# Attention probabilities and values in 32 bits: one product for three, one copy for two

## The reference, cut

```python
# cross-attention (layers 0 and 1): 16 heads of 16
scores = jnp.einsum('bhqd,bhkd->bhqk', Q, K) / SCALE
attn = jax.nn.softmax(scores, axis=-1)
out = jnp.einsum('bhqk,bhkd->bhqd', attn, V)
...
# layer 0's feed-forward attention: 16 heads of 64, values mixed from 8 experts
v = jnp.einsum('bthe,bted->bhtd', mix_v, proj_v)
scores = jnp.einsum('bhid,bhjd->bhij', q * scale, k)
probs = jax.nn.softmax(scores, axis=-1)
attn = jnp.einsum('bhij,bhjd->bihd', probs, v)
...
x = x + jnp.tanh(g_xattn[0]) * _L0_xattn_ref(_layernorm(x, axis=-1), ctx_1024, ctx_1024, ...)
x = x + jnp.tanh(g_ffn[0]) * _L0_ffn_ref(_layernorm(x, axis=-1), ...)
x = x + jnp.tanh(g_xattn[1]) * _L1_xattn_ref(_layernorm(x, axis=-1), ctx_1024, ctx_1024, ...)
x = x + jnp.tanh(g_ffn[1]) * _L1_ffn_ref(_layernorm(x, axis=-1), ...)
```

## Time and profile before

| | us |
|---|---|
| median of three runs | 1442.24 |
| lowest, highest | 1440.13, 1442.91 |
| span of the profiled execution | 1442.0 |

### The profile page before, as it was taken

How to read it: one execution, slowest core, us unless ns; L and a number is a source line. 1 busy time by engine, 2 the same in 40 slices (tenths; PEclk the granted TensorE clock), 3 DMA queues, 4 the chain that set the end, 5 groups by cost and what they waited for, 6 DMA issues and landing times. The chain is left out here.

```text
span 1442.0 us, 35263 instructions
## 1 busy us (share of the span) xinstructions
PE 1253.7 (87%) x13822; PEld 996.9 (69%) x13822; DVE 1135.6 (79%) x2068; ACT 903.7 (63%) x2071; POOL 278.4 (19%) x242
## 2 busy tenths in 40 slices
PE   1599998589989899889938999994699999999996
PEld 1376666367767767667725676763489999899995
DVE  5578887689999999999643777777688888888884
ACT  1477875158667677667624667663277677677762
POOL 2000000100000000000000000000236666666663
PEclk8689999799999999999666999995599999999998
DMA  8000000133452353352220000000867788778871
GB/s 231 12 9 9 6 2 2 41 93 74 114 146 67 101 151 76 100 151 73 68 66 9 5 9 5 2 2 1 290 225 227 227 249 245 222 231 250 234 189 30
DMA packets 172065, 152.96 MB, mean 106 GB/s; under 512 B 62589, under 2 KB 154386, under 8 KB 171906
## 3 DMA queue, kind: packets, MB, share of 16 engines
q1 hardware_dynamic: 151906, 129.51, 30.0%
q0 software_dynamic: 13936, 16.79, 6.1%
q10 hardware_dynamic: 6064, 4.46, 1.1%
HBM read 116.89 MB, written 36.70 MB: 107 GB/s over the span
## 5 line engine op out<-in xcount | busy, mean ns | idle before, releaser
L1857 POOL DMA_INDIRECT out<-m_yo,m_xg x70 | 161.5, 2307 | 135.9 <-DVE m_yo L1972 120.5
L1879 ACT ACTIVATE m_hf<-m_ps,m_bue 128x256 f32<-128x256 f32 x280 | 117.3, 471 | 106.5 <-PE m_ps L84 106.5
L82 PE MATMUL m_ps<-m_xt,m_us 128*128 128x256 f16 x560 | 153.7, 274 | 0.0
L83 PE MATMUL m_ps<-m_xt,m_us 128*128 128x256 f16 x560 | 153.7, 274 | 0.0
L84 PE MATMUL m_ps<-m_xt,m_us 128*128 128x256 f16 x560 | 153.6, 274 | 0.0
L82 PE MATMUL m_ps<-m_ds,m_hs 128*128 128x256 f16 x560 | 152.6, 273 | 0.3 <-DVE m_yo L1972 0.3
L84 PE MATMUL m_ps<-m_ds,m_hs 128*128 128x256 f16 x560 | 152.6, 273 | 0.0
L83 PE MATMUL m_ps<-m_ds,m_hs 128*128 128x256 f16 x560 | 152.6, 273 | 0.0
L473 ACT ACTIVATE x_pr<-x_ps,x_mx 128x120 f32<-128x120 f32 x512 | 143.3, 375 | 9.8 <-DVE x_mx L687 9.2
L1053 ACT ACTIVATE f_pr<-f_ps,f_nb 128x256 f32<-128x256 f32 x256 | 107.8, 477 | 66.0 <-DVE f_nb L1331 65.7
L481 ACT ACTIVATE x_pt<-x_ps 120x512 f16<-120x512 f32 x128 | 77.0, 602 | 86.2 <-PE x_ps L84 78.8
(11 more groups left out here) (367 smaller groups left out, 3832.7 us busy)
## 6 DMA issues: line engine op xcount, KB each, us to landing
m_uraw<-in_L_ffn_Wup SPq DMA_DIRECT2D x35, 1024.0 KB, 5.5
m_draw<-in_L_ffn_Wdown SPq DMA_DIRECT2D x35, 1024.0 KB, 5.8
head_values<-f_v_row SPq DMA_DIRECT2D x16, 520.0 KB, 5.5
f_vh<-head_values SPq DMA_DIRECT2D x16, 520.0 KB, 3.9
head_outputs<-f_at_row SPq DMA_DIRECT2D x16, 512.0 KB, 3.0
f_at_in_t<-head_outputs SPq DMA_DIRECT2D x16, 512.0 KB, 6.1
expert_values<-f_pv_row SPq DMA_DIRECT2D x8, 512.0 KB, 2.8
f_pv_in_t<-expert_values SPq DMA_DIRECT2D x8, 512.0 KB, 5.6
```

What stands on the lines that cost most here:

```text
L82: pe.matmul(out, lhs[0], rhs[0], start=(n == 0), stop=False)
L83: pe.matmul(out, lhs[0], rhs[1], start=False, stop=False)
L1857: pool.indirect_dma_start(rows_of, bass.IndirectOffsetOnAxis(xg[j % RING][:, ti, D:D + 1].bitcast(I32), 0), yo[j % 2][:, ti, :], None, bou ...
L1879: ins = act.activation(hf[:, q, m, :], U(q)[:, m, :], ACT.Gelu, bias=weights.bue[par][:, 2 * q + m:2 * q + m + 1], scale=UNSPLIT)
```

## The change

In all three attentions the transposed probabilities are copied from `PT` once, as 32-bit numbers, and the values are kept in 32 bits; each product of the two is one 32-bit matmul. In x0 and x1 the copies of even units are ScalarE's and those of odd units VectorE's, with a semaphore for each (`pt_copied`). In ffn all of them stay with ScalarE, VectorE's `pt_part` is gone, and so is `low` for the mixed values: the rows go to DRAM as soon as ScalarE has copied them (`act_high` in place of `low_done`), as many bytes as before (65 numbers of 4 bytes for 130 of 2). In x0 and x1 the values are made on VectorE in one step.

```diff
-        vf = two("vf", [SK, D])
-        va = two("va", [SK, 2, H, DK + 1], F16)
+        va = two("va", [SK, H, DK + 1])
...
-        pt = two("pt", [SK, 2, HG, P], F16)
+        pt = two("pt", [SK, HG, P])
...
             def pt_part(b, u):
+                if u % 2 == 1:
+                    return
                 n = XA_UNITS * b + u
                 act.wait_ge(pt_ready, n + 1)
                 if n >= 2:
                     act.wait_ge(pv_done, n - 1)
-                act.activation(pt[u % 2][:, 0], PT(u), ACT.Copy, scale=SPLIT).then_inc(pt_hi, 1)
+                act.activation(pt[0][:], PT(u), ACT.Copy).then_inc(pt_copied[0], 1)
...
-                    pe.wait_ge(pt_done, n - 1)
+                    pe.wait_ge(pt_copied[u % 2], n // 2)
...
-                pe.wait_ge(pt_done, XA_UNITS * b + u + 1)
+                pe.wait_ge(pt_copied[u % 2], (XA_UNITS * b + u) // 2 + 1)
                 for h, head in enumerate(heads(u)):
-                    last = matmul3(pe, O(ti)[:, head, :],
-                                   [(tuple(pt[u % 2][:, hl, h, :] for hl in range(2)),
-                                     tuple(va[b % 2][:, hl, head, :] for hl in range(2)))])
+                    last = pe.matmul(O(ti)[:, head, :], pt[u % 2][:, h, :], va[b % 2][:, head, :], start=True, stop=True)
...
-                    chain(dve.scalar_tensor_tensor(vf[par][:], front[0:SK, 0:D], 1.0 / SPLIT, s.bv[0:SK, layer, :],
-                                                   ALU.mult, ALU.add))
-                    v = vf[par][:].rearrange("k (h d) -> k h d", h=H)
-                    chain(dve.tensor_copy(va[par][:, 0, :, 0:DK], v))
-                    dve.tensor_tensor(va[par][:, 1, :, 0:DK], v, va[par][:, 0, :, 0:DK], ALU.subtract).then_inc(front_done, 1)
+                    by_head = lambda ap: ap.rearrange("k (h d) -> k h d", h=H)
+                    dve.scalar_tensor_tensor(va[par][:, :, 0:DK], by_head(front[0:SK, 0:D]), 1.0 / SPLIT,
+                                             by_head(s.bv[0:SK, layer, :]), ALU.mult, ALU.add).then_inc(front_done, 1)
...
             def pt_part(b, u):
-                dve.wait_ge(pt_hi, XA_UNITS * b + u + 1)
-                dve.scalar_tensor_tensor(pt[u % 2][:, 1], PT(u), SPLIT, pt[u % 2][:, 0],
-                                         ALU.mult, ALU.subtract).then_inc(pt_done, 1)
+                if u % 2 == 0:
+                    return
+                n = XA_UNITS * b + u
+                dve.wait_ge(pt_ready, n + 1)
+                if n >= 2:
+                    dve.wait_ge(pv_done, n - 1)
+                dve.tensor_copy(pt[1][:], PT(u)).then_inc(pt_copied[1], 1)
...
-LOW_KINDS = (F_PV, F_Q, F_K, F_MIXV)
+LOW_KINDS = (F_PV, F_Q, F_K)
...
-    v_d = nc.dram_tensor("head_values", (SQ, H, 2 * VW), F16).ap()
+    v_d = nc.dram_tensor("head_values", (SQ, H, VW), F32).ap()
...
-        pt = two("pt", [P, 2, TPB, TPB, P], F16)
+        pt = two("pt", [P, TPB, TPB, P])
...
-                sp.wait_ge(low_done, LOW[b, (F_MIXV, 2 * ti + 1)] + 1)
+                sp.wait_ge(act_high, HIGH[b, (F_MIXV, 2 * ti + 1)] + 1)
...
                 for ti in range(TPB):
-                    last = matmul3(pe, O(h)[:, h % 2, ti, :],
-                                   [(tuple(pt[h % 2][:, hl, c, ti, :] for hl in range(2)),
-                                     tuple(vh[b % 2][:, c, row, hl * VW:hl * VW + VW] for hl in range(2))) for c in range(TPB)])
+                    for c in range(TPB):
+                        last = pe.matmul(O(h)[:, h % 2, ti, :], pt[h % 2][:, c, ti, :], vh[b % 2][:, c, row, :],
+                                         start=(c == 0), stop=(c == TPB - 1))
...
-            def pt_part(b, h):
-                dve.wait_ge(pt_hi, H * b + h + 1)
-                dve.scalar_tensor_tensor(pt[h % 2][:, 1].rearrange("p c t q -> p (c t q)"), PT(h), SPLIT,
-                                         pt[h % 2][:, 0].rearrange("p c t q -> p (c t q)"),
-                                         ALU.mult, ALU.subtract).then_inc(pt_done, 1)
-
...
-                    earlier(b, h, FF_LAG - 1, pt_part)
```

More of the change, by code:

```diff
@@ L392, in xattn_stage @@
         pt_ready = sem("pt_ready")
-        pt_hi = sem("pt_hi")
-        pt_done = sem("pt_done")
+        pt_copied = [sem("pt_by_act"), sem("pt_by_dve")]
         pv_done = sem("pv_done")
@@ L424, in _ @@
             if layer == 1:
-                sp.wait_ge(ones_set, 6)
+                sp.wait_ge(ones_set, 4)
                 sp.dma_start(s.rows_in[0:1, :], zeros[0:1, :]).then_inc(rows_zeroed, 16)
@@ L432, in _ @@
             for par in range(2):
-                chain(pool.memset(va[par][:, 0, :, DK:DK + 1], 1.0))
-                chain(pool.memset(va[par][:, 1, :, DK:DK + 1], 0.0))
+                chain(pool.memset(va[par][:, :, DK:DK + 1], 1.0))
             chain(pool.memset(zeros[:], 0.0))
@@ L595, in _ @@
                 project(0, j)
-            pe.wait_ge(ones_set, 4)
+            pe.wait_ge(ones_set, 2)
             score(0, 0)
@@ L826, in ffn_stage @@
         spread_v = two("spread_v", [P, SPREAD, 4, TG, H8], F16)
-        v_row = sb("v_row", [P, GROUPS, 2, 2 * VW], F16)
-        vh = two("vh", [P, TPB, H, 2 * VW], F16)
+        v_row = sb("v_row", [P, GROUPS, 2, VW])
+        vh = two("vh", [P, TPB, H, VW])
         nb = two("nb", [P, TPB])
         pr = two("pr", [P, TPB, SQ])
-        pt = two("pt", [P, 2, TPB, TPB, P], F16)
+        pt = two("pt", [P, TPB, TPB, P])
         rs = two("rs", [P, 2 * TPB])
@@ L888, in parts_of @@
             rows = v_row[:, SPREAD * r:SPREAD * r + SPREAD].rearrange("p g x c -> p (g x) c")
-            return rows[:, :, 0:DH], rows[:, :, VW:VW + DH], 1.0 / SPLIT
+            return rows[:, :, 0:DH], None, 1.0 / SPLIT
         @block.sync
@@ L996, in _ @@
             chain(pool.memset(v_row[:, :, :, DH:DH + 1], 1.0))
-            chain(pool.memset(v_row[:, :, :, VW + DH:VW + DH + 1], 0.0))
             def rows(b):
@@ L1022, in pt_part @@
                     act.wait_ge(pv_done, n - 1)
-                act.activation(pt[h % 2][:, 0].rearrange("p c t q -> p (c t q)"), PT(h), ACT.Copy,
-                               scale=SPLIT).then_inc(pt_hi, 1)
+                act.activation(pt[h % 2][:].rearrange("p c t q -> p (c t q)"), PT(h), ACT.Copy).then_inc(pt_done, 1)
             def high(b, j):
@@ L1075, in back_hi @@
                 act.activation(zt[:, 0].rearrange("p c q -> p (c q)"), bank(use), ACT.Copy).then_inc(act_high, 1)
-            act.wait_ge(made, 6)
+            act.wait_ge(made, 5)
             for j in range(FF_FRONT - 1):
@@ L1146, in bank_left @@
                     pe.wait_ge(x_done, b + 1)
-                elif what == F_GATES:
+                elif what in (F_GATES, F_MIXV):
                     pe.wait_ge(act_high, HIGH[use] + 1)
@@ L1359, in _ @@
             normalised_x(0)
-            dve.wait_ge(made, 6)
+            dve.wait_ge(made, 5)
             chain(dve.tensor_copy(rank16[:], s.rank[:, E1 - E0:E1]))
```

## The result

The changed kernel takes 1572.3 us (median of four, 1567.4 to 1578.1) against 1442.5 us (with a fourth run of the kernel before); the ratio is 1.091, 95% interval 1.088 to 1.094. The forecast was 1524 us, the range 1488 to 1568. The direction was right, the size was not: +130 us for +82.

What follows compares the result with a forecast made beforehand. The prediction took TensorE to bound x0, x1 and nine steps of each ffn batch, and VectorE's chain steps 2 to 8. Terms x1 +35, x0 +23 and ffn +24 gave +82 us: 1524 us, range 1488 to 1568.

Steps and rivals of the forecast that it cites:

- the batch of x0: In x0, a steady batch was to go from 22.31 to 24.9 us, +2.6 for six batches; stage +23 us.
- The fourth rival: TensorE's granted clock falls to half level in parts of the attentions; put in ffn, +64 us, 1590 us, chance 0.05.
- TensorE idles less than before in every batch: The argument held against a fall of TensorE's granted clock in the attentions; no size of its own.
- x0 at full clock: x0's +23 us: +2.6 a batch for six, +4.4 for the first batch, +3 for the last.
- The price of the product: In all attentions, a 32-bit load-and-matmul pair takes 107 ns, eight pairs 0.856 us; +133 us of TensorE work.
- The first rival: The product's 32-bit load is as short as a transpose's, a pair 56 ns: 1428 us, faster; chance 0.12.
- the second: Rival: load and streaming do not overlap, a pair 121 ns in x, 161 in ffn: 1595 us; chance 0.07.
- What VectorE and ScalarE lose: Per batch: x, VectorE's pt_part 2.8 us, ScalarE's copies 2.4; ffn, VectorE's pt_part 10.9 and low parts 2.7.
- x1: In x1 TensorE has no idle time, so all added work shows: 8 × 4.43 less 0.5, +35 us.
- ffn: In ffn, +2.9 us a batch for six, +4 for the first batch, +3 for the last: +24 us.
- Steps 2 to 8: In an ffn batch, VectorE falls to 22.5 us, TensorE rises to 27.4; 28.99 becomes 27.7 us, −1.3.
- The nine other steps: In an ffn batch, where TensorE has next to no idle time: 9 × 0.484 = 4.4 us less 0.2.

Runs made afterwards that it cites:

- x_wide4: Changed kernel with each 32-bit product of x0 and x1 multiplying 68 columns in place of 17, same loads: 1502.9 us.
- x0_dense3: Changed kernel with three more 16-bit products of 480 columns per unit of x0, their results overwritten: 1546.2 us.
- x1_no_causal: Changed kernel with the three causal-mask products per unit of x1, and so the mask, left out: 1592.5 us.

## Why the prediction was wrong

*The step that failed is the batch of x0*, +86 us for +23. "x1 runs without gaps with a worse relation, so I take 24.9" took over the full clock of the earlier trace rows for TensorE in x0; the sum and the range have no term for the clock. The 24.9 us were right for full clock, but x0 has it in one batch of seven. What the clock costs is read from `x_wide4`, with the same products and loads at full clock: 316.4 − 244.1 = 72 us. `x0_dense3` brings the clock back in another way, and `x1_no_causal` takes it from x1.

The fourth rival had the mechanism, at a chance of 0.05 and put into ffn. That its 64 us are near the 72 is luck: ffn kept full clock in all its steady batches. Against it stood "TensorE idles less than before in every batch". That came true and argued nothing: the batches at 0.50 have a TensorE that is busy for every microsecond. What had changed is what it is busy with. In a unit of x0 twelve matmuls of 17 columns took 0.31 us; now eight take 0.81, and as their steps stay at 0.11 us with four times the columns (`x_wide4`), it is the loads that they last for.

*x0 at full clock* was put too high: +14 in `x_wide4` for +23. The steady batch is right (24.8 us, +2.5 for +2.6). But the first batch gained nothing, where +4.4 was put, and from the last batch's first maxima to ffn's it is 71.0 us for 71.1, where +3 was put.

*The price of the product* was right. The load was put at 105 ns from L1670 and the pair at 107; pairs follow each other at 112 ns, and eight take 0.81 us in x for the 0.856 of the sum, as the first step is short. The first rival (a load as short as a transpose's) is dead: 192 ns is the record, not 141. So is the second: eight pairs would have needed 0.97 us in x and 1.29 in ffn, and take 0.81 and 0.84.

*What VectorE and ScalarE lose* was right, and the price of VectorE's copy was put too low without effect: 0.69 us for 0.6, as long as the subtraction that it replaced.

*x1*, +27 for +35: 3.78 us a batch for 4.43, which is 3.9 us over six batches; most of that is the eight 32-bit pairs, priced at their full spacing. The first batch, partly at half clock before and after, took +1.5 where +4.4 was put.

*ffn*, +16 for +24. Steps 2 to 8 went from 28.99 to 26.15 us, −2.8, where −1.3 was worked out from "some 24 us of work" for TensorE plus 3.4. TensorE sets the pace there now (26.15 of 26.15 us), so its work was put some 1.3 us too high; that the tails of matmuls in its busy time are the reason is likely and not shown. The nine other steps went from 26.6 to 31.3, +4.7 for +4.2. That makes +1.85 a steady batch for +2.9. The first two batches took +7 and +3, and the end of the stage gave 2.9 us back where +3 was put: the last batch has full clock up to its last maxima now, for 0.72 before. So in ffn the change gave clock back.

Together: 82, less 9 in x0 at full clock, 8 in x1 and 8 in ffn, plus 72 of clock, is +129. The upper end of the range was short as well: a load of 114 ns for 105, in 2048 pairs, is +18 us, not +14. No row of before gives the size of the fall. x1 and x0 are the same loop with 24 causal products of difference, so that x0 was the one with less streaming in its time; that was the warning. These runs show that more streamed columns beside the same loads keep the clock and fewer lose it, and leave open how the chip weighs them.

## What to carry to other kernels

With a few moving columns a product costs its weight loads, and a 32-bit product has two loads, which follow each other at 112 ns, where 16-bit loads and matmuls follow each other at 25: count loads before counting products. Where TensorE sets the pace (a batch of x1, 28.9 us for 25.1), a relief of other engines bought nothing; where VectorE did (steps 2 to 8 of ffn, 26.1 for 29.0), it was worth even a dearer product, so divide a change by stretch and not only by stage. And when a change replaces streaming by loading, put the granted clock into the forecast as a term, with the time of the whole stage at the half level as its bound.

## What the hardware showed that was not expected

Added work made a kernel faster: 39 us of matmuls whose results nobody reads took 26 us off the time, and 51 more columns for each product took 70 us off, because the granted clock stayed at 2.4 GHz in the batches of x0. Work left out (the causal products) made it 20 us slower.

Columns of a 32-bit product were almost free up to 68: in place of 17 they lengthened a batch of 64 pairs by 0.16 us. With 256 columns (L1670) a pair takes 0.20 to 0.22 us for 0.11.

A change between matmuls that use 32 rows of the array and matmuls that use 120 or 128 costs about 0.1 us each way. It stands in the kernel before as well: the mask's product of 480 columns starts at 855.95 and is followed after 0.30 us by one that uses 32 rows, and the causal products of the same 480 columns follow each other after 0.20 us. The way back is the same: the transposes start 0.19 us after the last score matmul, and score matmuls follow each other after 0.10. The row after those of the earlier trace rows:

```profile
856.25 0.78 PE L550 MATMUL x_ps<-x_km,x_qt 32*128 32x240 f16 x6
```
